# A fifth tile size with its own code, a packed word of sizes, and a block-wise end in a routed feed-forward kernel

## The chip, the core and the metric

The kernel runs on one core of one Trainium2 chip. Its engines are TensorE (PE in the profile; PEld is its weight loads), VectorE (DVE), ScalarE (ACT), GpSimd (POOL) and SyncE (SP). The metric is device time in microseconds of one execution.

## The reference, cut to what matters

2,048 tokens of 256 values are turned by one matrix that depends on two quaternions and a gate, sent each to the best of eight experts, and the expert's output is added to the token.

```python
def _L0_ffn_ref(x, router_w, router_b, w1, b1, w2, b2):
    logits = jnp.einsum('bsd,de->bse', x, router_w) + router_b
    top1 = jnp.argmax(jax.nn.softmax(logits, axis=-1), axis=-1)
    out = jnp.zeros_like(x)
    for i in range(8):
        h = jnp.einsum('bsd,df->bsf', x, w1[i]) + b1[i]        # 256 -> 2048
        a, g = jnp.split(h, 2, axis=-1)
        y = jnp.einsum('bsh,hd->bsd', a * jax.nn.sigmoid(g), w2[i]) + b2[i]   # 1024 -> 256
        out = out + jnp.where((top1 == i)[..., None], y, 0.0)
    return out
x = x + _L0_ffn_ref(_L0_cond_ref(x, cond_256, q_right, gate), ...)
```

Evaluated on the inputs that it draws, the reference's own routing gives the experts 308, 336, 181, 195, 258, 268, 327 and 175 tokens.

## The kernel before

**The prologue.** SP loads the tokens in four parts (x_loaded) and the first expert's w1. TensorE spreads the quaternions (the matmuls into late_ps, L971), turns the tokens in eight pairs of blocks (the loop over f, L976 to L993), computes the logits (L999), and then rotates all tokens, 256 at a time, in rotate_blocks(0) to rotate_blocks(7) (L1018). ScalarE copies each rotated pair out of PSUM, and SP writes it to the DRAM buffer x_rows (L349). In the midst of this VectorE picks the expert of each token and counts them (L758 to L765, in_row); two small matmuls (L1034, L1035) turn the counts into ranks, and VectorE makes one-hot rows (slot_one_hot, L768) from which TensorE sums the row indices (L1051). TensorE's instructions run in program order, so rotate_blocks(2) and later stand behind L1034, which waits for in_row. GpSimd then gathers the first expert's rows from x_rows (gather(0), L438) after it has waited for x_rows_written (all eight writes) and idx_ready (the indices).

**The tiles.** Each expert is one tile of up to 512 columns. Its TensorE code is leaf(size): first_product makes eight chunks c of the two halves a and g, each from six matmuls (fp32 split in a high and a low part), then second_half makes two halves of the output from 24 matmuls each: 96 + 48 = 144 matmuls a tile. There is one leaf for each of SIZES = (224, 272, 336, 512); at "top" a tree of branches (by_size) picks the smallest size that holds the expert's count. ScalarE (sigmoid, L579, and u_hi, L585) and VectorE (gated, L854, and lo_u, L860) work at the width of a block class instead: 224 for two blocks of 128, 336 for three, 512 for four. The output of a tile is biased by ScalarE into yt (L593), turned back in the next tile's code (turn_back, L1120), added to the rows by VectorE and scattered by GpSimd (L452).

**The sizes.** VectorE writes a table ctrl, and in its last element a word with three bits for each of tiles 1 to 7 and an end mark of SPECIAL = 4. TensorE waits for ctrl_ready, loads three elements of ctrl (L1065, L1082, L1084) and shifts the word by three bits a tile.

**The visits.** A visit(line) branches to a label elsewhere in TensorE's program, from where a branch leads straight back. There are six of them, five in the prologue behind the first; their labels stand in the prologue (1), ahead of "top" (2), in the leaves of 224 (3), 272 (4 and 5) and 336 columns (6). visit(1) is the first thing that TensorE does.

**The end.** After the last tile the word gives the end mark, and the code at "special" waits for both halves of yt, turns all of them back in eight transposes, and adds one to y_turned. VectorE then adds block after block (L883), and GpSimd scatters each. "special" then branches to "done".

Of the kernel before, what the change touches and what calls it, by code (L numbers as in the profile page):

```python
# [5 lines left out]
def adaln_moe_ffn_kernel(nc, x, cond, q_right, gate, router_w, router_b, w1, b1, w2, b2, out):  # L6
# [16 lines left out]
    P = 128  # L23
# [15 lines left out]
    SIZES = (224, 272, 336, 512)  # L39
# [16 lines left out]
    SPECIAL = len(SIZES)  # L56
# [8 lines left out]
    with ctx:  # L65
# [40 lines left out]
        ctrl = sb("ctrl", 3 + TAB, I32)  # L106
# [8 lines left out]
        places = sb("places", NE)  # L115
# [74 lines left out]
        turn_ps = pair[0] + pair[1]  # L190
        early_ps, late_ps = y_half
# [42 lines left out]
        ctrl_ready = sem("ctrl_ready")  # L234
        rot_x_ready = sem("rot_x_ready")
# [21 lines left out]
        y_turned = sem("y_turned")  # L257
        last_added = sem("last_added")
# [105 lines left out]
        def _(pool):  # L364
# [32 lines left out]
            for e in range(NE):  # L397
                nc.gpsimd.memset(places[:, e:e + 1], float(1 << (LEFT * (e - 1))) if e > 0 else 0.0)
# [106 lines left out]
        def _(act):  # L505
# [49 lines left out]
            for h in range(KH):  # L555
                act.sem_inc(yt_done[h], 1)
            act.sem_inc(sig_done[NC - 2], 1)
# [46 lines left out]
            def gate_tile(i, e, n):  # L604
# [35 lines left out]
        def _(dve):  # L640
# [164 lines left out]
            def indices(idx_ps, at, count):  # L805
# [13 lines left out]
            steps = sm[:, 6 * NE:7 * NE]  # L819
            bigger = ct[:, 0:NE * MORE].rearrange("p (e m) -> p e m", m=MORE)  # L820
# [5 lines left out]
            left = sm[:, 7 * NE + SPARE:7 * NE + SPARE + 1]  # L826
# [7 lines left out]
            V.memset(ctrl[:, 1 + TAB:2 + TAB], 0)  # L834
            link(V.tensor_tensor(places[:, :], places[:, :], steps, ALU.mult))
            link(V.tensor_reduce(left, places[:, :], AX.X, ALU.add))
            V.tensor_scalar(ctrl[:, 2 + TAB:3 + TAB], left, float(SPECIAL << (LEFT * (NE - 1))), None, ALU.add)\
                .then_inc(ctrl_ready, 1)
# [24 lines left out]
            def rows_of(i, first, count):  # L863

                return (pairs[buffer_of(i)].rearrange("p (s k h d) -> p s k h d", s=NSUB, k=2, h=KH)[:, first:first + count, 1],
                        y_ps[:, :].rearrange("p (h s d) -> p s h d", h=KH, s=NSUB)[:, first:first + count])

            def add_rows(i):

                for s in range(NSUB):  # L870
                    dve.wait_ge(gathered[s], (i + 1) * 16)
                dve.wait_ge(y_turned, i + 1)
                rows, y = rows_of(i, 0, NSUB)
                V.tensor_tensor(rows, y, rows, ALU.add).then_inc(y_done, 1)  # L874

            def add_last(i, blocks):

                for s in range(blocks):
                    dve.wait_ge(gathered[s], (i + 1) * 16)
                dve.wait_ge(y_turned, i + 1)  # L880
# [46 lines left out]
            for i in range(NE, TAB):  # L927
                with dve.If(last_tile >= i):
# [4 lines left out]
                    add_rows(i)  # L933

        @block.tensor
        def _(pe):
# [20 lines left out]
            def landing(line):  # L957
                here = nc.cur_bb
                pe.br(f"past{line}")
                nc.switch_bb(f"landing{line}", parent=visited_from[line])  # L960
                pe.nop()
                pe.br(f"back{line}")
                nc.switch_bb(f"past{line}", parent=here)

# [344 lines left out]
```

## Time and profile before

| | us |
|---|---|
| median of 3 runs (lowest, highest) | 208.42 (208.19, 209.0) |
| the profiled execution | 207.35 |
| its span | 205.6 |

An execution's time is its span and 1.75 us around it. The profiled execution lies 1.07 us (0.5%) below the median of the runs. In the rows below, a time is in microseconds from the span's start unless it says ns, PE rows are TensorE's matmuls, "q" behind an engine's name is its sequencer (branches, waits, register work), and [a <-b] behind an instruction is the idle time of its engine before it and what ended that. The matmuls' durations overlap, so their pitch is read from starts.

### The profile page before, as it was taken

Reading aid. Unit: us, or ns where it says so; the run is one execution under the profiler, and the core shown is the slowest. Engines: PE = TensorE matmul, PEld = TensorE weight load, DVE = VectorE, ACT = ScalarE, POOL = GpSimd, SP = SyncE. Lnnn points to the kernel's source line nnn. Section 1 sums busy time; section 2 is a strip of 40 time slices with the busy share of each in tenths; the row PEclk is TensorE's granted clock in tenths of the full one; section 3 lists DMA queues with packets and bytes.
Section 4 is the critical chain, followed back from the end, with each engine's and each line's share of the span. In section 5 each row is a group of like instructions: output and inputs, shape, how many; then the busy total and the mean of one; then the engine's idle time right before and its main releaser. Section 6 shows DMA issues by size and latency. Waiting matters only on the chain.

```text
span 205.6 us, 4304 instructions
## 1 busy us (share of the span) xinstructions
PE 191.6 (93%) x1451; PEld 181.2 (88%) x1453; DVE 146.1 (71%) x296; ACT 125.1 (61%) x222; POOL 87.7 (43%) x138
## 2 busy tenths in 40 slices
PE   7997867999999999999999999999999999999960
PEld 3777733999999999999999999999999999999950
DVE  4928944678854888398869869995999488839510
ACT  2454770385756676486875958695777667648310
POOL 8002544631700645445467084555637364004403
PEclk9999999999999999999999999999999999999997
DMA  4999925879948161787198469618861976001001
GB/s 136 383 402 385 311 64 190 261 260 328 308 128 357 51 213 47 249 333 238 34 390 302 154 199 406 232 38 303 344 205 53 336 277 208 0 0 37 28 5 43
DMA packets 20054, 42.34 MB, mean 206 GB/s; under 512 B 2472, under 2 KB 14905, under 8 KB 17978
## 3 DMA queue, kind: packets, MB, share of 16 engines
q1 hardware_dynamic: 15808, 31.54, 42.8%
q0 software_dynamic: 4000, 10.50, 16.1%
q8 instruction: 8, 0.13, 0.3%
q14 instruction: 20, 0.16, 0.2%
q10 hardware_dynamic: 218, 0.01, 0.1%
HBM read 35.74 MB, written 8.13 MB: 213 GB/s over the span
## 4 chain that ended last, share of the span: by engine, by line
PE 90%; DMA 4%; issue 1%; DVE 1%; POOL 1%; ACT 1%; DVEq 0%; POOLq 0%
PE y_ps L1208 8%; PE g_ps L1176 8%; PE g_ps L1169 8%; PE a_ps L1169 8%; PE y_ps L1210 8%; PE a_ps L1176 8%; PE y_ps L1209 8%; PE a_ps L1172 8%; PE g_ps L1172 8%; PE y_ps L1120 3%; PE y_ps L942 3%; DMA x_turn<-x_rows,g_idx 2%; PE a_ps L1018 2%; PE a_ps L1099 2%; DMA x_rows<-arena 2%
## 5 line engine op out<-in xcount | busy, mean ns | idle before, releaser
L854 DVE SCALAR_TENSOR_TENSOR arena<-a_ps,b_t,arena 128x336 f32<-128x336 f32 (+1 forms) x64 | 33.3, 521 | 27.7 <-PE a_ps L1176 24.1
L579 ACT ACTIVATE arena<-g_ps,b_t 128x336 f32<-128x336 f32 (+1 forms) x64 | 32.2, 503 | 32.4 <-PE g_ps L1176 32.2
L452 POOL DMA_INDIRECT out_dram<-x_turn,s_idx x22 | 28.5, 1295 | 47.3 <-DVE x_turn L874 35.4
L740 DVE TENSOR_TENSOR w_lo<-w_raw,w_hi 128x1024 fp32r<-128x1024 f32 x32 | 37.7, 1221 | 9.1 <-DMA x_turn<-x_rows,g_idx 5.2
L438 POOL DMA_INDIRECT x_turn<-x_rows,g_idx x24 | 30.6, 1275 | 31.1 <-DMA out_dram<-x_turn,s_idx 17.3
L1208 PE MATMUL y_ps<-u_hi,w_hi 128*128 128x336 f32 (+2 forms) x128 | 38.1, 298 | 0.3 <-issue 0.3
L1210 PE MATMUL y_ps<-u_lo,w_hi 128*128 128x336 f32 (+2 forms) x128 | 37.5, 293 | 0.0
L1209 PE MATMUL y_ps<-u_hi,w_lo 128*128 128x336 f32 (+2 forms) x128 | 37.5, 293 | 0.0
L1169 PE MATMUL g_ps<-xr_hi,w_hi 128*128 128x336 f32 (+2 forms) x128 | 36.1, 299 | 0.0
L1169 PE MATMUL a_ps<-xr_hi,w_hi 128*128 128x336 f32 (+2 forms) x128 | 35.6, 294 | 0.0
L1172 PE MATMUL a_ps<-xr_hi,w_lo 128*128 128x336 f32 (+2 forms) x128 | 35.5, 293 | 0.0
L1172 PE MATMUL g_ps<-xr_hi,w_lo 128*128 128x336 f32 (+2 forms) x128 | 35.5, 293 | 0.0
L585 ACT ACTIVATE u_hi<-arena 128x336 fp32r<-128x336 f32 (+1 forms) x64 | 28.4, 444 | 10.6 <-DVE arena L854 10.6
L528 ACT ACTIVATE w_hi<-w_raw 128x1024 fp32r<-128x1024 f32 x32 | 32.0, 1059 | 0.0
L860 DVE TENSOR_TENSOR u_lo<-arena,u_hi 128x336 fp32r<-128x336 f32 (+1 forms) x64 | 29.2, 456 | 1.2 <-ACT u_hi L585 0.5
L1176 PE MATMUL g_ps<-xr_lo,w_hi 128*128 128x336 f32 (+2 forms) x128 | 27.3, 294 | 0.0
L1176 PE MATMUL a_ps<-xr_lo,w_hi 128*128 128x336 f32 (+2 forms) x128 | 27.2, 293 | 0.0
L1208 PEld LDWEIGHTS y_ps<-u_hi,w_hi 128*128 128x128 f32 x128 | 24.2, 189 | 0.4 <-issue 0.4
L1169 PEld LDWEIGHTS g_ps<-xr_hi,w_hi 128*128 128x128 f32 x128 | 24.2, 189 | 0.3 <-issue 0.3
L1172 PEld LDWEIGHTS g_ps<-xr_hi,w_lo 128*128 128x128 f32 x128 | 24.3, 190 | 0.0
L1172 PEld LDWEIGHTS a_ps<-xr_hi,w_lo 128*128 128x128 f32 x128 | 24.3, 190 | 0.0
L1209 PEld LDWEIGHTS y_ps<-u_hi,w_lo 128*128 128x128 f32 x128 | 24.3, 190 | 0.0
(181 smaller groups left out, 306.8 us busy)
## 6 DMA issues: line engine op xcount, KB each, us to landing
w_raw<-in_L_ffn_w_dram SPq DMA_DIRECT2D x16, 1024.0 KB, 7.9
w_raw<-in_L_ffn_w_dram SPq DMA_DIRECT2D x16, 512.0 KB, 4.6
x_own<-in_x_dram SPq DMA_DIRECT2D x4, 512.0 KB, 6.0
x_rows<-x_own SPq DMA_DIRECT2D x4, 512.0 KB, 11.1
x_rows<-arena SPq DMA_DIRECT2D x8, 256.0 KB, 3.4
x_turn<-x_rows,g_idx POOLq DMA_INDIRECT x24, 6.0
out_dram<-x_turn,s_idx POOLq DMA_INDIRECT x22, 3.7
x_own<-x_rows,g_idx POOLq DMA_INDIRECT x8, 5.6
```

The lines of the kernel that those rows point to most:

```text
L438: nc.gpsimd.indirect_dma_start(out=pairs[buffer_of(i)][:, s * ROW:(s + 1) * ROW], out_offset=None, in_=x_rows, in_offset=bass.IndirectOffs ...
L528: nc.scalar.activation(unit_of(w1_hi, u), raw_unit(u), ACT.Copy)\
L579: nc.scalar.activation(sig[:, c % SIG_RING, 0:n], pair[c % RING][1][:, 0:n], ACT.Sigmoid, bias=b1_t[:, bass.ds(e * (2 * NC) + (NC + c), 1) ...
L740: V.tensor_tensor(unit_of(w1_lo, u), raw_unit(u), unit_of(w1_hi[:, :].bitcast(F32), u), ALU.subtract)\
L854: V.scalar_tensor_tensor(u32[:, c % (8 - SIG_RING), 0:n], pair[c % RING][0][:, 0:n], b1_t[:, bass.ds(e * (2 * NC) + c, 1)], sig[:, c % SIG ...
L860: V.tensor_tensor(u_lo[:, at:at + n], u32[:, c % (8 - SIG_RING), 0:n], u_hi[:, at:at + n].bitcast(F32), ALU.subtract).then_inc(u_lo_done[c ...
L1169: one = T.matmul(dst, w_part(w1_hi, k), xh, start=(k == 0), stop=False)
L1172: T.matmul(dst, w_part(w1_lo, k), xh, start=False, stop=False)
L1176: last = T.matmul(dst, w_part(w1_hi, k), xr_lo[:, k * ITEM:k * ITEM + n], start=False, stop=(k == KH - 1))
L1208: T.matmul(dst, w2_hi[:, wv], u_hi[:, uv], start=(c == 0), stop=False)
L1209: T.matmul(dst, w2_lo[:, wv], u_hi[:, uv], start=False, stop=False)
L1210: last = T.matmul(dst, w2_hi[:, wv], u_lo[:, uv], start=False, stop=(c == NC - 1))
```

## The change

- SIZES gets 320 between 272 and 336. TensorE has five leaves; the classes of width for ScalarE and VectorE stay 224, 336 and 512.
- The word of sizes holds all eight tiles, as 5 minus the size's number, with 0 as the end mark. VectorE makes it ahead of the rest of the table, from five small operations, before the one-hot rows for spare tiles (q_oh_spare); it signals packed_ready. TensorE loads this one word. It reads ctrl only in "special".
- visit(1) stays, with its label behind the leaf of 272 columns and so ahead of that of 320. The other five visits and their labels go. The five warming matmuls behind visit(1) go, and so do two of the four long ones ahead of the first tile.
- The two matmuls for wr_rot move from f == 4 to f == 6.
- rotate_blocks(2) and (3) move ahead of the matmuls that wait for in_row.
- At the end, ScalarE biases the first half of the output as soon as it is there, and the second half in two parts: 128 columns, signalled by yt_first, and the rest. TensorE turns the first half back (half_turned), and then the second half block by block, each block into a PSUM bank of its own. VectorE adds the first half for all blocks in one operation, and then the second half block by block.

```diff
-    SIZES = (224, 272, 336, 512)
+    SIZES = (224, 272, 320, 336, 512)
...
+    PLACES = [1 << (LEFT * e) for e in range(NE)]
...
+        apart = turn_ps[0:NSUB]
...
             def biased_rest(i, e, n):
...
                 if i >= NE - 1:
-                    for h in range(KH):
-                        biased(i, e, h, 0, FIRST, yt_done[h])
+                    biased(i, e, 0, 0, min(n, FIRST), yt_done[0])
+                    biased(i, e, 1, 0, P, yt_first)
+                    biased(i, e, 1, P, min(n, FIRST), yt_done[1])
...
             indices(early_ps[:, 0:FX], 0, FX)
-            subtile_one_hot(q_oh_spare, FX, TS - FX, q_spare).then_inc(q_oh_spare_ready, 1)
-
-            dve.wait_ge(spare_ready, 1)
...
             link(V.tensor_tensor(bigger, cnt.unsqueeze(2).to_broadcast([P, NE, MORE]), ...
             link(V.tensor_reduce(steps, bigger, AX.X, ALU.add))
+            link(V.tensor_tensor(places[:, :], places[:, :], steps, ALU.mult))
+            link(V.tensor_reduce(left, places[:, :], AX.X, ALU.add))
+            V.tensor_scalar(packed[:, :], left, float(len(SIZES) * sum(PLACES)), None, ALU.add).then_inc(packed_ready, 1)
+            subtile_one_hot(q_oh_spare, FX, TS - FX, q_spare).then_inc(q_oh_spare_ready, 1)
+
+            dve.wait_ge(spare_ready, 1)
...
+            def add_by_block(i, blocks, done):
...
+                dve.wait_ge(half_turned, i - NE + 2)
+                V.tensor_tensor(rows[:, 0:blocks, 0], y_half[0][:, 0:blocks * P].rearrange("p (s d) -> p s d", d=P),
+                                rows[:, 0:blocks, 0], ALU.add)
                 for s in range(blocks):
-                    rows, y = rows_of(i, s, 1)
-                    V.tensor_tensor(rows[:, 0], y[:, 0], rows[:, 0], ALU.add).then_inc(last_added, 1)
+                    dve.wait_ge(block_turned, (i - NE + 1) * NSUB + s + 1)
+                    last = V.tensor_tensor(rows[:, s, 1], apart[s][:, 0:P], rows[:, s, 1], ALU.add)
...
             visit(1)
             pe.wait_ge(still_set, 1)
-            keep_warm(early_ps, 5)
...
-                if f == 3:
-                    visit(2)
-                if f == 4:
+                if f == 6:
                     pe.wait_ge(wr_loaded, 16)
...
-                if g == 2:
-                    visit(3)
...
-            rotate_blocks(1)
+            for b in range(1, GROUPS):
+                rotate_blocks(b)
             pe.wait_ge(consts_ready, CONSTS)
             pe.wait_ge(in_row_ready, 1)
...
-            for b in range(2, NB // 2):
+            for b in range(GROUPS, NB // 2):
                 rotate_blocks(b)
-                if b == 5:
-                    visit(4)
...
-            visit(5)
...
             keep_warm_long(late_ps, 2)
-            pe.wait_ge(ctrl_ready, 1)
-            last_tile = load_last(pe)
-            visit(6)
-            keep_warm_long(late_ps, 2)
+            pe.wait_ge(packed_ready, 1)
...
-            pe.reg_load(word_reg, ctrl[0:1, 1:2])
-            pe.reg_mov(size_reg, f_size(reg(word_reg, 127)))
-            pe.reg_load(left_reg, ctrl[0:1, 2 + TAB:3 + TAB])
+            pe.reg_load(left_reg, packed[0:1, 0:1])
+            pe.reg_mov(size_reg, reg(left_reg, 1 << 30) & ((1 << LEFT) - 1))
+            pe.reg_mov(left_reg, reg(left_reg, 1 << 30) >> LEFT)
...
                     leaf(low)
                     here = nc.cur_bb
                     pe.br("top")
+                    if low == 1:
+                        landing_behind(1)
...
             nc.switch_bb("special", parent=begin)
             tile = reg(tile_reg, TAB)
-            turn_back_rows(NSUB)
+            pe.wait_ge(yt_done[0], at1)
+            for s in range(NSUB):
+                last = T.transpose(y_half[0][:, s * P:(s + 1) * P], yt[:, s * P:(s + 1) * P], ident[:, :])
+            last.then_inc(half_turned, 1)
+            for s in range(NSUB):
+                if s < 2:
+                    pe.wait_ge((yt_first, yt_done[1])[s], at1)
+                T.transpose(apart[s][:, 0:P], yt[:, ITEM + s * P:ITEM + (s + 1) * P], ident[:, :]).then_inc(block_turned, 1)
+            pe.wait_ge(ctrl_ready, 1)
+            last_tile = load_last(pe)
...
             first16 = pe.to_reg(reg(tile_reg, TAB) * 16 + 16)
+            pe.wait_ge(y_done, at1)
```

## Rows read from the trace of the kernel before

**Rows 1.** The page: busy time of TensorE; its granted clock in 40 slices.
```profile
PE 191.6 (93%) x1451; PEld 181.2 (88%) x1453; DVE 146.1 (71%) x296; ACT 125.1 (61%) x222; POOL 87.7 (43%) x138
PEclk9999999999999999999999999999999999999997
```

**Rows 2.** Groups by form, line L1208 at 336 columns.
```profile
L1208 PE MATMUL y_ps<-u_hi,w_hi 128*128 128x336 f32 x48 | 15.4, 320 | 0.0
```

**Rows 3.** Chain that ended last (start, us, what): chunks at 336, then at 272 columns.
```profile
44.53 0.31 PE g_ps L1176 x2
45.45 0.31 PE a_ps L1176 x2
...
125.02 0.25 PE g_ps L1176 x2
125.78 0.25 PE a_ps L1176 x2
```

**Rows 4.** Timeline of VectorE, the last chunk of tile 0.
```profile
51.32 0.57 DVE L854 SCALAR_TENSOR_TENSOR arena<-a_ps,b_t,arena 128x336 f32<-128x336 f32 x1 [0.55 <-PE a_ps L1176]
```

**Rows 5.** Timeline of TensorE at the wait for in_row.
```profile
17.96 0.17 PE L1034 MATMUL g_ps<-in_row,lower 128*128 128x8 bf16 x1 [1.36 <-DVE in_row L765]
```

**Rows 6.** Chain that ended last, from the rotations to the first gather.
```profile
20.94 0.89 PE g_ps L1018 x8
...
24.28 3.30 DMA x_rows<-arena
...
28.46 4.51 DMA x_turn<-x_rows,g_idx
```

**Rows 7.** Windows: length, busy PE, PEld, DVE, ACT, POOL, PEclk, DMA share, GB/s.
```profile
22.00:24.00 2.00, 2.00 (x18) 1.78 (x16) 2.00 (x10) 1.41 (x3) 1.57 (x5) 1.00 0.73 242
24.00:26.00 2.00, 1.07 (x17) 0.68 (x16) 1.88 (x10) 2.00 (x4) 0.00 (x0) 1.00 1.03 348
```

**Rows 8.** Timeline of VectorE from the ranks to the first indices.
```profile
18.46 0.17 DVE L777 COPY sm<-g_ps 128x8 f32<-128x8 f32 x1
...
21.73 3.60 DVE L768 TENSOR_SCALAR work<-iota,r_f,tok 128x128 f16<-128x128 bf16 x15
...
25.68 0.19 DVE L807 TENSOR_SCALAR g_idx<-y_ps 128x32 int32<-128x32 f32 x1
```

**Rows 9.** Three lines' instructions: branch durations in ns (min/median/max), first and last start.
```profile
L954 PEldq COMPARE_BRANCH  x5: 175/287/381, 7.1 to 29.1; - x5
L1261 PEldq COMPARE_BRANCH  x1: 3408/3408/3408, 198.3 to 198.3; - x1
L1245 PEldq COMPARE_BRANCH  x8: 169/169/184, 56.4 to 195.4; - x8
```

**Rows 10.** Timeline of TensorE at the start of the program.
```profile
1.50 2.31 PE L942 MATMUL y_ps<-still 128*128 128x512 bf16 x5 [1.50 <-DVE still L651]
3.75 1.03 PE L971 MATMUL y_ps<-ident,scratch 13*128 13x16 f32 x4
...
7.67 0.96 PE L983 MATMUL g_ps<-ident,x_own 128*128 128x128 f32 x4
8.46 0.63 PE L983 MATMUL a_ps<-ident,x_own 128*128 128x128 f32 x4
```

**Rows 11.** Chain that ended last, the end.
```profile
197.49 0.55 ACT yt L593
198.17 1.08 PE y_ps L1120 x8
199.38 0.43 DVE x_turn L883
...
200.08 0.98 POOL out_dram L452
```

**Rows 12.** Groups by form: ScalarE on 144 columns, VectorE on 128.
```profile
L721 DVE TENSOR_TENSOR scratch<-mask_j,coef_t 128x128 f32<-128x128 f32 x2 | 0.5, 290 | 0.0
...
L551 ACT ACTIVATE b_t<-y_ps 128x144 f32<-128x144 f32 x1 | 0.3, 285 | 0.0
```

More of the change, by code:

```diff
@@ L105, in adaln_moe_ffn_kernel @@
         s_idx = sb("s_idx", TAB * NSUB, I32)
-        ctrl = sb("ctrl", 3 + TAB, I32)
+        ctrl = sb("ctrl", 2 + TAB, I32)
+        packed = sb("packed", 1, I32)
+        places = sb("places", NE)
         ident = sb("ident", P)
@@ L397, in _ @@
             for e in range(NE):
-                nc.gpsimd.memset(places[:, e:e + 1], float(1 << (LEFT * (e - 1))) if e > 0 else 0.0)
+                nc.gpsimd.memset(places[:, e:e + 1], -float(PLACES[e]))
             for m, size in enumerate(SIZES[:-1]):
@@ L814, in _ @@
             indices(early_ps[:, 0:FX], 0, FX)
[L815 to L817 removed]
             MORE = len(SIZES) - 1
             steps = sm[:, 6 * NE:7 * NE]
+            left = sm[:, 7 * NE + SPARE:7 * NE + SPARE + 1]
             bigger = ct[:, 0:NE * MORE].rearrange("p (e m) -> p e m", m=MORE)
@@ L833, in _ @@
             V.tensor_scalar(ctrl[:, 1 + NE:1 + TAB], owner, float(MORE), None, ALU.add)
[L834 to L838, printed above, removed]
+            V.memset(ctrl[:, 1 + TAB:2 + TAB], 0).then_inc(ctrl_ready, 1)
             dve.wait_ge(idx_spare_summed, 1)
@@ L861, in lo_u, with rows_of @@
                                 u_hi[:, at:at + n].bitcast(F32), ALU.subtract).then_inc(u_lo_done[c], 1)
-            def rows_of(i, first, count):
-                return (pairs[buffer_of(i)].rearrange("p (s k h d) -> p s k h d", s=NSUB, k=2, h=KH)[:, first:first + count, 1],
-                        y_ps[:, :].rearrange("p (h s d) -> p s h d", h=KH, s=NSUB)[:, first:first + count])
+            def rows_of(i):
+                return pairs[buffer_of(i)].rearrange("p (s k h d) -> p s k h d", s=NSUB, k=2, h=KH)[:, :, 1]
             def add_rows(i):
@@ L1122, in turn_back, with turn_back_rows @@
                 return last
-            def turn_back_rows(blocks):
+            def turn_back_rows():
                 for h in range(KH):
                     pe.wait_ge(yt_done[h], at1)
-                turn_back(range(blocks)).then_inc(y_turned, 1)
+                turn_back(range(TURNED)).then_inc(y_turned, 1)
             def turn_back_rest():
@@ L1233, in leaf, with jump, by_size @@
                 second_half(size, 1)
-            def by_size(size, low, high):
-                if low == high:
-                    if low == SPECIAL - 1:
-                        with pe.If(size >= SPECIAL):
-                            here = nc.cur_bb
-                            pe.br("special")
-                            nc.switch_bb("behind_special", parent=here)
+            def jump(to, behind):
+                here = nc.cur_bb
+                pe.br(to)
+                nc.switch_bb(behind, parent=here)
+            def by_size(code, low, high):
+                if low == high:
                     leaf(low)
@@ L1248, in by_size @@
                 middle = (low + high + 1) // 2
-                with pe.If(size < middle):
-                    by_size(size, low, middle - 1)
+                with pe.If(code > len(SIZES) - middle):
+                    by_size(code, low, middle - 1)
                 with pe.Else():
-                    by_size(size, middle, high)
+                    if middle == high == len(SIZES) - 1:
+                        with pe.If(code < 1):
+                            jump("special", "behind_special")
+                    by_size(code, middle, high)
             begin = nc.cur_bb
@@ L1257, in _ @@
             tile = reg(tile_reg, TAB)
-            turn_back_rows(NSUB)
-            with pe.If(last_tile < tile):
-                here = nc.cur_bb
-                pe.br("done")
-                nc.switch_bb("behind_done", parent=here)
-            pe.reg_load(word_reg, ctrl[0:1, bass.ds(tile + 1, 1)])
-            pe.reg_mov(size_reg, f_size(reg(word_reg, 127)))
-            pe.reg_mov(left_reg, SPECIAL)
+            pe.wait_ge(yt_done[0], at1)
[8 more added lines that the diff above has]
+            last_tile = load_last(pe)
+            with pe.If(last_tile < tile):
+                jump("done", "behind_done")
+            pe.reg_mov(size_reg, 1)
+            pe.reg_mov(left_reg, 0)
             pe.reg_mov(held_reg, NE)
```

42 lines of the change are left out of this document (17 added, 25 removed).

## The prediction

> **What bounds the kernel now.** I read the page first. TensorE is busy for 93% of the span and stands at its higher clock level, 2.4 GHz, in 39 of 40 slices [rows 1]. The chain of waits then shows where that matters. From the first tile's first chunk to the last tile's last half it is TensorE alone, chunk behind chunk at an even pitch [rows 3], so a tile costs what its 144 matmuls cost, and all that VectorE, ScalarE and the queues do there is hidden. Only two stretches lie outside: the prologue, in which the chain goes from the rotations to the writes of x_rows to the gather [rows 6], and the end, in which it steps from ScalarE to TensorE, VectorE and GpSimd [rows 11]. The edits fall into these three places, and what one place gains is not lost again in another, since each is in series with the next.
>
> **The leaf of 320 columns.** The group at 336 columns has 48 matmuls of a kind that each tile runs 16 times (two halves by eight chunks), so three tiles run at 336 [rows 2]. They are the experts with 308, 336 and 327 tokens; only the first fits into 320. So one tile of eight changes its leaf. Its price from the pitch of six matmuls: 0.92 us at 336 columns (44.53 to 45.45) and 0.76 us at 272 (125.02 to 125.78) [rows 3], that is 0.0025 us a column for the six, 0.04 us for 16 columns, and 24 groups of six in a tile: 24 x 0.04 = **0.96 us less**. VectorE and ScalarE keep their width of 336 there. In the tile's last chunk VectorE still waited 0.55 us for TensorE [rows 4], while TensorE will come some 0.6 us earlier by then (sixteen groups by 0.04); so VectorE is just kept busy, and the second product's order gives the last chunk some 3 us more before it is read (seven of eight steps of three matmuls, half of 0.92 us each). I count the 0.96 in full; the lower bound is half of it.
>
> **Pairs 2 and 3 early.** TensorE stood idle for 1.36 us before L1034, waiting for in_row [rows 5]. Two pairs of rotations at 0.89 us [rows 6] fill this and 0.42 us more. So the last pair is done 1.36 us earlier, and the ranks come 0.42 us later. What does each end at? The writes of x_rows end at 27.58 (24.28 + 3.30), and the gather starts at 28.46 [rows 6]. The DMA engines were at a share of 0.73 in 22 to 24 us and at 1.03 right behind [rows 7]: 2 us x 0.30 = 0.6 us of transfers could move up, and not much more, since the engines are then full. By the GB/s of the two windows it would be (348 - 242) x 2 / 348 = 0.6 too. So the writes can gain about 0.65 us; the upper bound is that the last ones land quicker too, and they gain what the rotations do. The indices: after the ranks VectorE works without a pause to the first indices at 25.68 + 0.19 = 25.87 [rows 8]; with 0.42 us more that is 26.3, still ahead of 26.9.
>
> **One visit, and what goes with it.** The five visits that go cost the sequencer 0.18 to 0.38 us a branch [rows 9], next to matmuls that were queued or waits: I count nothing for them, nor for the table's loads that TensorE drops, since all of this ended before the gather landed (28.46 + 4.51). The visit that stays goes to a place behind two leaves. The trace of before has one branch to code that nothing had touched, the one to "done", and it took 3.41 us against 0.29 us for a visit [rows 9]. I take that: 3.1 us more at the very start. TensorE's first matmul was at 1.50, and L971 at 3.75, behind five warming matmuls of 2.31 us together [rows 10]. These go, and L971 can start at 1.50 + 3.1 = 4.6, so 0.85 us later; its followers (five warming matmuls, the turns) shift by as much. The clock softens this: the four transposes at 7.67 took 0.96 us and those at 8.46 took 0.63 [rows 10], so the step up from 1.2 to 2.4 GHz lay between. If it comes at the same time again, the turns that are 0.85 us late run mostly at the higher level, and only about 0.2 us is lost; if it comes 0.85 us later as well, all of it is. I take **0.6 us lost**. Bounds: nothing (the target is there already), and 1.5 us, if the step comes so late that some five groups more cost 0.33 us extra each. Moving the wr matmuls to f == 6 costs nothing, as the copies of the turned tokens wait for the same engine in either order; it keeps TensorE from waiting for rot_t, which is late by the same 0.85 us.
>
> **The start in sum.** The last rotation is 1.36 - 0.6 = 0.76 us earlier, the writes by the smaller of this and their own limit, **0.65 us**; the indices are at 25.87 + 0.42 + 0.6 = 26.9, level with the writes at 27.58 - 0.65 = 26.9. The gather, the turns and the first chunk follow in step. The bounds: 1.36 - 1.5, and with the ranks' 0.42 on top of 1.5 the indices at 27.8, so 0.2 us later; and 1.36 - 0.2, so 1.2 us earlier.
>
> **The word of sizes.** Five small VectorE operations now stand ahead of q_oh_spare, about 1 us, and so TensorE's sums for spare tiles and its two long warming matmuls come 1 us later. They end well before the gather lands. Nothing on the path; TensorE's sparse time grows, which is rival C.
>
> **The end.** Before: ScalarE's yt from 197.49 for 0.55, eight transposes from 198.17 for 1.08, VectorE's first block at 199.38 for 0.43, GpSimd's first scatter at 200.08 [rows 11]. After: the first half is biased long before, its transposes follow the last product directly, and VectorE adds it (256 columns, 0.43) at about 197.85 to 198.3. ScalarE's first 128 columns take 0.29 (144 columns took 0.285 [rows 12]) to 197.78. The steps between engines as before (0.13 us to TensorE, 0.13 to VectorE, 0.27 to GpSimd), one transpose 0.3, one block of 128 columns 0.29 [rows 12]: 197.78 + 0.13 + 0.3 + 0.13 = 198.34, + 0.29 + 0.27 = 198.90. **1.18 us less**, bounds 0.9 and 1.3. The second scatter follows the first at GpSimd's own pace. "special" then loads ctrl and branches to "done", again 3.4 us: until about 202.7, while the second scatter is issued from 200.2 on and has to land; hidden, though thinly.
>
> **The sum.** 0.65 + 0.96 + 1.18 = 2.8 us. Against the profiled execution 207.35 - 2.8 = 204.55; the runs' median lies 1.07 us above that execution, so 208.42 - 2.8 = **205.6 us**.
>
> **Rivals.**
>
> A. *The start gives nothing* (0.16). The step up of the clock comes a stage later: 1.5 us lost against 1.36 gained. 0.96 + 1.18 - 0.1 = 2.0 us: 206.4. For it: the step is the one thing in the rows whose time the kernel does not set. Against: the warming matmuls behind L971 remain.
>
> B. *320 is not worth 16 columns*, because VectorE, with no idle time left in tile 0, becomes the bound (0.05): 0.5 us of the 0.96 is lost, 206.1. Against it: TensorE reads the last chunk some 3 us later.
>
> C. *TensorE's clock falls before the first tile* (0.07). From the end of the rotations, about 22.5, to the long warming matmuls at about 28.7, it has only small matmuls, and two of the four long ones are gone. At the end of the trace, with the engine idle, the clock does fall (the last slice has 7 [rows 1]). Against: before, its idle gaps of 1.36 us and less brought no fall. Price: the turns, the warming matmuls between them and the first chunk at half pace, about 1.5 us: 207.1. The Trainium skill (TensorE: Matmul & The Clock Gate, Part 1: The HAM clock gate) has the low clock as the default state, which activity releases and an idle engine gets back; by that rule the thinner prologue is the risky edit here, and the trace agrees so far that the clock falls once the engine has nothing left.
>
> D. *The program no longer stays in TensorE's instruction memory* (0.09): slower. Five leaves instead of four, and five visits that touched them are gone. A branch to absent code costs 3.41 us [rows 9]. The sequencer takes the branch back to "top" at 195.4, 2.1 us before ScalarE gets the last result at 197.49 [rows 9, 11], so a miss at a tile's switch costs 3.4 - 2.1, about 1.4 us. Two misses eat the 2.8 us, from the third on it is slower; at all seven switches 7 x 1.4 = 9.8 us: 215.4. For it: the program grows by a quarter. Against: before, the chain goes from tile to tile within TensorE [rows 3], and a leaf of 272 columns runs for 24 x 0.76 = 18 us, in which the next stretch can come. The Trainium skill (Runtime: NRT & Kernel Launch, Instruction fetch mechanics) gives TensorE room for 2,048 instructions and says that a taken branch out of it stalls; five leaves of 288 matmul and load instructions and the some 600 others that ran before (1451 + 1453 less 8 x 288 [rows 1]) make 2,040 by estimate, and waits and branches come on top. By that page the misses are likelier than I make them; the trace shows only the one at "done".
>
> **The numbers.** The forecast has 0.63, A 0.16, B 0.05, C 0.07, D 0.09. A measurement of this kernel tells about 0.5%, 1.04 us, from no change. All but D are faster by more than that, but for the ends of A and C together: faster 0.85, same 0.06, slower 0.09. The range: best ends 1.2 + 1.0 + 1.3 = 3.5 us, 204.9, and the runs scatter some 0.3 us below their median: 204.6. Above, it takes in A and C up to 207.3, which leaves D and a little of C and of the lower side out.
>
> **What would show it.** L1034 without an idle time of 1.36 us before it; a branch of about 3.4 us at the start and L971 near 4.6; the gather near 27.8; one group of matmuls at 320 columns, 16 of a line, with a pitch of 0.88 us; the first scatter about 1.2 us nearer to the last product. Wrong would make it: gaps of TensorE between tiles (D), a granted clock below 1 after 8.5 us (C), or turns at the slow pace beyond 9.5 us (A).

## The result, and the profile after

The changed kernel takes 214.63 us (median of 4 runs, 213.8 to 215.34), the kernel before beside it 208.71 us (208.19 to 210.08): 1.0272 times as long, with an interval of 1.0209 to 1.0335. The forecast was 205.6 us, faster; the kernel became slower by 5.9 us between the medians. The profiled execution took 215.34 us, its span is 213.0 us, 7.4 us more than before.

The page of the changed kernel, its clock row and its row for the queue of instruction packets, q8 (packets, MB, share of the engines):

```profile
PE 193.0 (91%) x1443; PEld 182.9 (86%) x1443; DVE 146.4 (69%) x297; ACT 125.4 (59%) x223; POOL 87.4 (41%) x139
...
PEclk9999988757999999999999999999999999999997
...
q8 instruction: 11, 0.18, 0.4%
```

TensorE's work is about as before [rows 1], but the clock is below full in slices 6 to 10 (about 27 to 53 us), where it was not before. Instruction packets on q8 number 11; the page of before has 8 of them, 0.13 MB. In both the size is 16 KB a packet (0.18 MB by 11). The page doesn't say which engine's instructions they hold; where they fall is told below.

The rows of two lines of the changed kernel: L952, the branch of the one visit, and L1244, the branches of the tree that picks a leaf (durations in ns, min/median/max, first and last start):

```profile
L952 PEldq COMPARE_BRANCH  x1: 3489/3489/3489, 0.9 to 0.9; - x1
L1244 PEldq COMPARE_BRANCH  x21: 65/88/4638, 37.6 to 205.7; - x21
```

The first answers to the visits and to "done" [rows 9]: 3.49 us, as forecast. The second was not forecast. One of 21 branches takes 4.64 us, and it is the first, at 37.6 us: the way into the leaf of 320 columns for tile 0. In the trace, a packet of q8 starts inside each of the two long branches, at 1.84 and at 39.58 us.

The chain that ended last, of the changed kernel (start, us, what):

```profile
24.92 3.75 DMA x_rows<-arena
...
29.55 1.25 POOL x_turn L444
...
32.41 4.91 DMA x_turn<-x_rows,g_idx
37.37 0.33 PE a_ps L1095
...
38.45 4.07 issue
42.52 0.61 PE g_ps L1163
...
44.99 1.12 issue
46.11 0.43 PE a_ps L1163
...
206.94 0.45 PE y_ps L1258 x4
207.51 0.42 DVE x_turn L889
207.94 0.41 DVE x_turn L893 x2
208.41 0.98 POOL out_dram L458
```

The gather starts at 29.55, 1.09 us later than before [rows 6]; its third part lands at 37.32 (32.41 + 4.91), where the trace of before has 34.99. Then TensorE stands for 4.07 us with all its data there ("issue": nothing in the profile that it waits for), and again for 1.12 us inside the first chunk, right behind another packet of q8 (43.67 to 44.61). Windows of the changed kernel (columns as in [rows 7]; PEclk is the figure behind POOL's):

```profile
36.00:38.00 2.00, 0.63 (x4) 0.46 (x5) 1.14 (x1) 0.27 (x1) 0.00 (x0) 1.00 0.38 111
...
40.00:42.00 2.00, 0.00 (x0) 0.00 (x0) 0.27 (x1) 0.00 (x0) 1.67 (x2) 0.53 1.07 378
42.00:44.00 2.00, 1.48 (x6) 1.51 (x7) 0.00 (x0) 0.00 (x0) 1.43 (x2) 0.50 0.88 283
...
50.00:52.00 2.00, 2.00 (x15) 2.00 (x14) 1.45 (x3) 0.56 (x2) 1.50 (x2) 0.91 0.62 195
```

In the idle gap, at 40.1 us, the clock falls from 2.4 to 1.2 GHz, and tile 0 runs at half pace from its first product until about 50.4 us.

The account needs the third gather and the starts of tiles 0 and 1. Of the kernel before, GpSimd's and TensorE's timelines, and the third part's time from issue to landing; of the changed kernel, TensorE's timeline at tile 1 (its tile 0 is in the chain above):

```profile
31.32 1.00 POOL L438 DMA_INDIRECT x_turn<-x_rows,g_idx  x1 [0.30 <-issue]
...
36.14 0.39 PE L1169 MATMUL g_ps<-xr_hi,w_hi 128*128 128x336 f32 x1
...
59.14 0.32 PE L1169 MATMUL g_ps<-xr_hi,w_hi 128*128 128x336 f32 x1
```

```profile
DMA to landing us min/median/max: 3.7/3.7/3.7
```

```profile
68.61 0.32 PE L1163 MATMUL g_ps<-xr_hi,w_hi 128*128 128x336 f32 x1
```

Tile 0 starts at 42.52 in place of 36.14 (+6.38: 2.33 by the third gather, 4.05 by the gap). Tile 0 lasts 26.09 in place of 23.00 (+3.09). The other seven tiles last as long as before, within 0.03 us each. From the last product to the end of the span it is 6.06 in place of 8.17 (-2.11). The sum is +7.36 of the 7.38 by which the spans differ.

### The profile page after: what moved, and what is told of

It is laid out like the page before. It is cut to its first block, busy times and chain, and to the rows that moved or that the text cites. A ratio compares the mean times of both kernels' runs of the same rounds, so it can differ in the third digit from the quotient of the medians.

```text
span 213.0 us, 4271 instructions
## 1 busy us (share of the span) xinstructions
PE 193.0 (91%) x1443; PEld 182.9 (86%) x1443; DVE 146.4 (69%) x297; ACT 125.4 (59%) x223; POOL 87.4 (41%) x139
## 4 chain that ended last, share of the span: by engine, by line
PE 84%; DMA 8%; issue 4%; POOL 2%; ACT 1%; DVE 0%; SPq 0%; DVEq 0%; POOLq 0%
PE g_ps L1163 8%; PE a_ps L1163 8%; PE g_ps L1170 8%; PE a_ps L1166 8%; PE g_ps L1166 8%; PE a_ps L1170 8%; PE y_ps L1202 8%; PE y_ps L1203 8%; PE y_ps L1204 8%; DMA x_own<-in_x_dram 4%; DMA x_turn<-x_rows,g_idx 2%; PE y_ps L1116 2%; PE a_ps L1024 2%; DMA x_rows<-arena 2%; PE g_ps L1024 2%
## 5 line engine op out<-in xcount | busy, mean ns | idle before, releaser
L444 POOL DMA_INDIRECT x_turn<-x_rows,g_idx x24 | 29.9, 1247 | 30.0 <-DMA out_dram<-x_turn,s_idx 17.1
L1163 PE MATMUL g_ps<-xr_hi,w_hi 128*128 128x224 f32 (+3 forms) x128 | 36.7, 302 | 4.1 <-issue 4.1
L1202 PE MATMUL y_ps<-u_hi,w_hi 128*128 128x224 f32 (+3 forms) x128 | 38.0, 297 | 0.3 <-issue 0.3
L1204 PE MATMUL y_ps<-u_lo,w_hi 128*128 128x224 f32 (+3 forms) x128 | 37.4, 292 | 0.0
L1203 PE MATMUL y_ps<-u_hi,w_lo 128*128 128x224 f32 (+3 forms) x128 | 37.4, 292 | 0.0
L1163 PE MATMUL a_ps<-xr_hi,w_hi 128*128 128x224 f32 (+3 forms) x128 | 35.9, 296 | 1.1 <-issue 1.1
L1166 PE MATMUL a_ps<-xr_hi,w_lo 128*128 128x224 f32 (+3 forms) x128 | 36.0, 297 | 0.0
L1166 PE MATMUL g_ps<-xr_hi,w_lo 128*128 128x224 f32 (+3 forms) x128 | 36.0, 297 | 0.0
L1170 PE MATMUL g_ps<-xr_lo,w_hi 128*128 128x224 f32 (+3 forms) x128 | 27.6, 297 | 0.0
L1170 PE MATMUL a_ps<-xr_lo,w_hi 128*128 128x224 f32 (+3 forms) x128 | 27.5, 297 | 0.0
L1163 PEld LDWEIGHTS a_ps<-xr_hi,w_hi 128*128 128x128 f32 x128 | 24.8, 194 | 0.0
```

What stands on the lines that cost most here:

```text
L444: nc.gpsimd.indirect_dma_start(out=pairs[buffer_of(i)][:, s * ROW:(s + 1) * ROW], out_offset=None, in_=x_rows, in_offset=bass.IndirectOffs ...
L1163: one = T.matmul(dst, w_part(w1_hi, k), xh, start=(k == 0), stop=False)
L1166: T.matmul(dst, w_part(w1_lo, k), xh, start=False, stop=False)
L1170: last = T.matmul(dst, w_part(w1_hi, k), xr_lo[:, k * ITEM:k * ITEM + n], start=False, stop=(k == KH - 1))
L1202: T.matmul(dst, w2_hi[:, wv], u_hi[:, uv], start=(c == 0), stop=False)
L1203: T.matmul(dst, w2_lo[:, wv], u_hi[:, uv], start=False, stop=False)
```

## The experiments

Three theories were tried. *Not there*: a leaf's code has to be touched shortly before its use and in order; the five visits did that, and the one far visit doesn't. *Too large*: five leaves don't fit, whatever is visited. *Clock by itself*: the thinner prologue lets the clock fall. All ratios below are to runs of the kernel before on the same chip, with their intervals. The runs are spread over two chips, on which the median of the kernel before lies between 208.09 and 209.42 us, so kernels are compared by these ratios. Line numbers in rows are each kernel's own.

**e1_visits_back.** Visits 2 to 6 and the six labels back in the changed kernel:

```diff
+                if f == 3:
+                    visit(2)
...
+                if g == 2:
+                    visit(3)
...
+                if b == 5:
+                    visit(4)
...
+            landing(1)
...
+            visit(5)
...
+            visit(6)
+            LANDING_AT = {(0, 7): 3, (1, 2): 4, (2, 3): 6}
...
+                if size == 1:
+                    landing(5)
...
-                    if low == 1:
-                        landing_behind(1)
...
+            landing_behind(2)
```

> The changed kernel with the kernel before's visits 2 to 6 and their six labels put back (visit(1) again to a label in the prologue); five sizes, pairs, end and word as changed; none of the dropped warming matmuls. Theory 'not there' (the code of a leaf has to be touched shortly before, in the order in which the program runs; the one far visit at the start leaves nothing behind): no branch of 3.5 us at 0.9 us, no branch of 4.6 us ahead of tile 0, tile 0 back at 22 us (23.0 less 0.96), the prologue 3 to 4 us shorter than in the changed kernel; 205.6 to 207 us. Theory 'too large' (five leaves do not fit whatever is visited): the 4 us gap ahead of or in tile 0 stays, or moves to another tile; 210 us or more. Theory 'clock by itself' (the prologue is too thin without the warming matmuls): the branches are short again, yet the granted clock still falls before or in tile 0; 207 to 209 us.

205.35 us (204.64 to 205.81), ratio 0.9825 [0.9762, 0.9887]. The visits' branches in e1, and its clock row:

```profile
L971 PEldq COMPARE_BRANCH  x5: 168/287/1568, 6.9 to 28.6; - x5
...
PEclk9999966999999999999999999999999999999998
```

No visit but the last, beside the wait for the gather, takes longer than before [rows 9]; there is no gap of 4 us, and tile 0 starts at 36.39. *Too large* falls: five leaves, and 0.9825 where the changed kernel has 1.0272. *Not there* holds for tile 0. Its label 6, counted by the leaf's number, now stands in the leaf of 320 columns, tile 0's own, as it stood in tile 0's own leaf of 336 before. The leaf of 336, tile 1's, lies right behind that of 320 in the program; no visit touches it in e1, and tile 1 doesn't wait. The clock falls nevertheless (27.4 to 34.2 us).

**e2_visits_warm.** e1 with the dropped warming matmuls back:

```diff
+            keep_warm(early_ps, 5)
...
+            keep_warm_long(late_ps, 2)
```

> As the run before it (visits 2 to 6 back), and the five warming matmuls at the start and the two long ones ahead of the first tile put back as well. 'Not there': same as the run before within 0.5 us if the clock fell only because of the stall; 205 to 206 us. 'Clock by itself': 1.5 to 3 us faster than the run before, and the granted clock stays at 1.00 from 8.5 us on. 'Too large': no better than 210 us.

206.24 us, ratio 0.9887 [0.9848, 0.9927]: not faster than e1. The clock falls here too (26.1 to 32.9 us), so putting the dropped warming matmuls back doesn't keep it up.

**e3_no_visit.** The changed kernel without its visit:

```diff
-            visit(1)
...
-                    if low == 1:
-                        landing_behind(1)
```

> The changed kernel without its one visit; nothing put back. 'Not there': the visit bought nothing, so the gap of about 4 us ahead of tile 0's first product stays as it is, while the start is up to 3 us earlier: 211.5 to 213.5 us. If the visit did bring in part of the leaf, the gap grows by what it had saved, or a second one shows in another tile, and the time is 214 us or more. 'Too large' expects the gap as well, and says nothing on the start.

Three runs took 224.2 to 224.9 us and one 209.75; the profile is of one of the long ones (224.22). The tree's branches there:

```profile
L1241 PEldq COMPARE_BRANCH  x21: 65/92/7423, 34.3 to 214.8; - x21
```

Tile 0 waits for its leaf as in the changed kernel (4.27 us at 34.3), and tile 1 for its own, the 336, twice in a row (5.34 us at 62.2 and 7.42 at 67.6). So the one visit did not serve tile 0. In the long run that has a trace tile 1 is worse off without it, against "bought nothing"; e10 shows such a double wait again. The fourth run, 209.75 us, is close to the kernel before on that chip (209.42), with a mean granted clock of 0.973 against 0.934 to 0.939 in the three. It has no trace; it may be that such stalls differ from run to run of one kernel, and what the one visit was worth is left open by this.

**e4_no_512.** The changed kernel without the leaf of 512 columns:

```diff
-                    leaf(low)
+                    if low < len(SIZES) - 1:
+                        leaf(low)
```

> The changed kernel, with its one visit, but TensorE's code for tiles of 512 columns left out (no tile has that size with these inputs, so the work done is the same); the program is then about as long as before the change. 'Too large': with room for four leaves the branch ahead of tile 0 is short and the time falls to 206 to 208 us. 'Not there': length does not matter, the branch of 4.6 us ahead of tile 0 stays, 213 to 215.5 us.

213.25 us, ratio 1.0168 [1.0084, 1.0251]. The tree's branches:

```profile
L1245 PEldq COMPARE_BRANCH  x21: 65/88/4687, 37.5 to 204.8; - x21
```

The same stall with four leaves, as *not there* expected (213 to 215.5 us). *Too large* falls a second time.

**e9_far_before.** The kernel before, and of the whole change its visits alone:

```diff
-                if f == 3:
-                    visit(2)
...
-            landing(1)
...
-            visit(6)
...
-            LANDING_AT = {(0, 7): 3, (1, 2): 4, (2, 3): 6}
+            LANDING_AT = {}
...
+                    if low == 1:
+                        landing_behind(1)
...
-            landing_behind(2)
```

> The kernel before with its four sizes, prologue, pairs, warming matmuls and end, and only its visits changed: visit(1) goes to a label behind the leaf of 272 columns, the other five are gone. If the visits alone are the cause: a branch of about 3.5 us at 0.9 us, a branch of about 4.6 us ahead of tile 0 (now to the leaf of 336, the one behind the label), 211 to 214 us, 1.5 to 2.5 % slower than the kernel before. If the fifth leaf is needed for the loss: the start costs up to 1 us, tile 0 does not wait, 208.5 to 210 us.

214.43 us (213.86 to 215.36), ratio 1.0293 [1.0245, 1.0341]: the loss of the change, with four leaves and every warming matmul in place, and a little above the expected 211 to 214 us. The visit's branch, the tree's branches, and TensorE's timeline at the first product:

```profile
L935 PEldq COMPARE_BRANCH  x1: 3262/3262/3262, 0.9 to 0.9; - x1
L1240 PEldq COMPARE_BRANCH  x18: 65/77/4363, 38.1 to 205.2; - x18
```

```profile
42.76 0.62 PE L1160 MATMUL g_ps<-xr_hi,w_hi 128*128 128x336 f32 x1 [3.70 <-issue]
```

**e11_far_and_near.** e1 with the far label for visit(1):

```diff
-            landing(1)
...
+                    if low == 1:
+                        landing_behind(1)
```

> e1_visits_back with visit(1) to its far place again, that is the changed kernel with visits 2 to 6 put back. With e1 (near ones alone), the changed kernel (far one alone) and e3 (none) it makes a square. If the near visits decide: tile 0 does not wait, and what is left is the price of the far visit at the start, first rotations 1 to 1.5 us later than in e1, 206.5 to 208 us. If the far visit throws out what the near ones need: the branch of 4 us or more is there again, 210 us or more.

211.71 us, ratio 1.0146 [1.0091, 1.0201]. Neither theory: tile 0 doesn't wait, but the first near visit does, and the start is 6 us late. The near visits' branches, and TensorE's timeline at that one:

```profile
L971 PEldq COMPARE_BRANCH  x5: 174/289/6140, 8.4 to 35.3; - x5
```

```profile
15.00 1.10 PE L999 MATMUL a_ps<-ident,x_own 128*128 128x128 f32 x4 [4.16 <-issue]
```

Behind the far visit, visit(2) takes 6.14 us, where e1 has a short one; that the far visit takes away what the next one reaches for is the reading of this, not a thing that a row shows. In the square, the near ones alone have the ratio 0.9825, both 1.0146, the far one alone 1.0272, and none three long runs and one of 209.75 us (e3). The traces divide more plainly than the times: tile 0 waits for its leaf in the two without the near visits, and in neither of the two with them.

**e10_late_visit.** The changed kernel with its visit behind the last wait ahead of the tiles:

```diff
-            visit(1)
...
             pe.wait_ge(yt_set, 1)
+            visit(1)
```

> The changed kernel with its one visit moved from the start of the program to the last instructions ahead of the loop over the tiles, where TensorE waits for the gather. If what counts is that the code is touched shortly before its use: the 3.5 us leave the start (2 to 3 us won there), the same 3.5 us are paid next to the wait for the gather, and the branch ahead of tile 0 is short: 206.5 to 209 us. If code that is read in between, or the order of the visits, decides: the branch ahead of tile 0 takes 4 us or more all the same, 211 to 215 us.

219.21 us, ratio 1.0488 [1.0421, 1.0556]. The visit's branch, the tree's branches, and TensorE's timeline ahead of tile 1:

```profile
L971 PEldq COMPARE_BRANCH  x1: 3411/3411/3411, 29.1 to 29.1; - x1
L1244 PEldq COMPARE_BRANCH  x21: 65/92/7443, 35.2 to 209.4; - x21
```

```profile
57.96 0.31 PE L1204 MATMUL y_ps<-u_lo,w_hi 128*128 128x320 f32 x1
69.80 0.62 PE L1163 MATMUL g_ps<-xr_hi,w_hi 128*128 128x336 f32 x1 [11.53 <-issue]
```

Half of the theory held: 3.41 us next to the wait for the gather cost nothing, tile 0 starts at 36.10 and doesn't wait. Then tile 1 waits for 11.53 us, as in e3, and the time lies above both expected ranges. This late touch served tile 0's leaf and not tile 1's. With the visits of before and of e1 no tile waits.

**e6_320_and_end.** The kernel before with the fifth size and the end by block (the change's parts at biased_rest, add_by_block and "special"):

```diff
-    SIZES = (224, 272, 336, 512)
+    SIZES = (224, 272, 320, 336, 512)
...
+            def add_by_block(i, blocks, done):
```

> The kernel before with only the fifth size and the end by block; its visits, prologue, warming matmuls, pairs and word as before. The prediction's two other terms: tile 0 at 22.0 us in place of 23.0 and the first scatter 1.2 us nearer to the last product, 2.1 us less than the kernel before, clock at 1.00 up to the end. 'Too large' (five leaves do not fit): one tile or more starts 3 us late. If the start's edits were worth the 0.65 us of the prediction, e5 is that much faster than this one; if the pairs bring nothing because the writes end with the queue, both are the same within 0.3 us.

205.54 us (204.54 to 206.1), ratio 0.9837 [0.98, 0.9874]. Its clock fell as well, in 26.5 to 29.9 us, with the prologue of before, and tile 0 still starts at 36.12. No tile starts late, so *too large* falls here too. By the ratio it gains 3.4 us, where the two terms of the prediction sum to 2.1.

**e12_end_only.** e6 without the fifth size:

```diff
-    SIZES = (224, 272, 320, 336, 512)
+    SIZES = (224, 272, 336, 512)
```

> The kernel before with the end by block alone; four sizes. Predicted term: the first scatter 1.18 us nearer to the last product. The scatters' landing decides the rest: 1.2 us less in all if the last landing comes as long after its issue as before the change (3.5 us), about 2.3 us less if it comes after 2.3 to 2.6 us as in the changed kernel. 206 to 207.5 us; and e6 is 0.5 to 1 us faster than this, the worth of the fifth size.

205.76 us, ratio 0.9882 [0.9841, 0.9923], 2.3 us less than the kernel before it (208.09) by the medians, as expected where the last scatter lands sooner, and just under the range of 206 to 207.5 us. What the fifth size adds to it (0.5 to 1 us expected) is not settled by the times: the medians of e6 and e12 differ by 0.22 us, their ratios by 0.45%, and the intervals overlap. In the traces tile 0 takes 22.51 us in e6 and 23.44 in e12. Two rows on the last scatters, from issue to landing, of before and of e12:

```profile
DMA to landing us min/median/max: 2.8/3.2/3.5
```

```profile
DMA to landing us min/median/max: 2.3/2.5/2.8
```

**e5_warm_between.** e1 with warming matmuls in the thin stretch:

```diff
+            keep_warm(late_ps, 2)
             pe.wait_ge(b1_t_done, 1)
...
             pe.wait_ge(still32_set, 1)
+            keep_warm_long(late_ps, 3)
             pe.wait_ge(q_oh_spare_ready, 1)
```

> As e1_visits_back (visits 2 to 6 back), with warming matmuls in the two places where TensorE has little left: two bf16 ones behind the rotations, ahead of the wait for the biased b1, and three long ones ahead of the wait for q_oh_spare (the gap of 1.9 us in e1 and e2). Theory 'thin stretch' (the granted clock fell at 26 to 27 us in e1 and e2 because the rotations now end 1.5 us earlier against the indices and q_oh_spare comes 0.9 us later): the clock stays at 1.00 to the end, tile 0 takes 22.0 us, and its first product comes about 3.2 us after the first gather landed, as before the change, in place of 4.3 (e1): 1 to 1.5 us faster than e1. Theory 'no cost' (the warming and the gather hide the low clock): same as e1 within 0.5 us.

206.19 us, ratio 0.9862 [0.9824, 0.99]. The clock falls all the same (26.5 to 29.9 us), and there is no gain over e1. Since the warming did not keep the clock up, this says nothing on what the fall costs: "no cost" is not shown by it.

**e7_word_late.** e1 with q_oh_spare ahead of the word's five operations again:

```diff
+            subtile_one_hot(q_oh_spare, FX, TS - FX, q_spare).then_inc(q_oh_spare_ready, 1)
             MORE = len(SIZES) - 1
...
-            subtile_one_hot(q_oh_spare, FX, TS - FX, q_spare).then_inc(q_oh_spare_ready, 1)
```

> As e1_visits_back, with q_oh_spare written ahead of the five operations for the word of sizes, as before the change. 'Thin stretch' with the word as its cause: TensorE's gap ahead of the sums for spare tiles falls from 1.9 to about 1.0 us and the granted clock stays at 1.00 or falls later and for less long, 0.5 to 1.3 us faster than e1. With the pairs as its cause: the gap is shorter and the clock falls all the same, same as e1.

206.26 us, ratio 0.9883 [0.9838, 0.9929]. The gap shrank from 1.89 to 0.99 us, the clock fell later and for less long (27.4 to 30.8 us); the time is not better than e1's.

**e8_pairs_late.** e1 with one pair ahead of the wait for in_row:

```diff
-            for b in range(1, GROUPS):
-                rotate_blocks(b)
+            rotate_blocks(1)
...
-            for b in range(GROUPS, NB // 2):
+            for b in range(2, NB // 2):
```

> As e1_visits_back, with pairs 2 and 3 back behind the wait for in_row. 'Thin stretch' with the pairs as its cause: the rotations end near 24 us again, the clock stays at 1.00 in 24 to 34 us, and the first gather starts within 0.2 us of e1's, since the writes end with the queue either way: 0.5 to 1.3 us faster than e1. If the pairs' early place is worth the predicted 0.65 us: the gather starts 0.65 us later, and the time is 0.3 to 0.7 us more than e1's unless the clock gives it back.

206.03 us, ratio 0.9846 [0.9789, 0.9902]: no difference to e1. The clock fell later, at 33.0, and this once it touched the turns: tile 0 starts 1.94 us after the third gather has landed, where before it took 1.15.

The chain of e7, which has the pairs early and nearly the start of before, at the last pair and in two chunks of tile 0:

```profile
21.08 0.91 PE g_ps L1034 x8
...
22.01 0.61 ACT arena L554
...
22.75 4.52 DMA x_rows<-arena
...
28.15 4.42 DMA x_turn<-x_rows,g_idx
...
38.24 0.15 PE g_ps L1183
...
39.12 0.15 PE a_ps L1183
```

and VectorE's timeline of e7 in the last chunk of tile 0:

```profile
50.31 0.57 DVE L861 SCALAR_TENSOR_TENSOR arena<-a_ps,b_t,arena 128x336 f32<-128x336 f32 x1 [0.31 <-PE a_ps L1190]
```

They are read in the next section.

## Why the prediction was wrong, by its own steps

**The step that failed** is "The five visits that go cost the sequencer 0.18 to 0.38 us a branch ... I count nothing for them". It priced the visits by their branches and left out what they do. Short branches [rows 9] did not say that the visits were idle, but that each found its target there. The square shows what the near visits do: with them tile 0 has no gap, without them it has. e9 shows the whole edit of the visits by itself: without the five, and with the far one, the kernel before loses 2.9%. e1 shows the reverse: with the near ones the changed kernel is 1.75% faster than the kernel before. The far visit bears a part of the loss of its own, which the prediction, with 0.6 us lost at the start, didn't count either: beside the near ones it takes the ratio from 0.9825 to 1.0146, by the 6.14 us at visit(2) (e11). Which of the five near visits is needed was not tried. That e1's 205.35 us is so close to the forecast of 205.6 is in part luck: the term for the start was too large and that for the end too small, as told below, and e1 ran on a chip where the kernel before took 209.42 us. Against the kernel before, 1.3% was forecast.

**Rival D** (0.09) named the mechanism, code that TensorE has to wait for, with the wrong cause and the wrong place. The cause was "five leaves instead of four"; e4 has four leaves and stalls, e1 and e6 have five and don't. The place was every switch of tiles, 1.4 us each behind a running product; it was the first entry, at 37.6 us, where TensorE has nothing queued and the whole branch is seen. Its price there: 4.07 + 1.12 us of gaps, and 26.09 - 22.00 - 1.12 = 2.97 us for the half pace (22.00 is what tile 0 takes in e7, below). The rival's own difference was off as well: 3.4 - 2.1 is 1.3 us, not 1.4. The Trainium skill (Runtime: NRT & Kernel Launch, Instruction fetch mechanics) calls the instruction memory a FIFO that is filled sequentially in blocks of 16 KiB, and has a taken branch out of what was read ahead stall. The packets of 16 KB and the stalls in e4, e9 and e11 agree with that; which blocks each visit leaves behind, and why tile 1 waits twice in e3 and e10, no run here shows.

**The visit at the start** was priced rightly in itself: 3.49 us against 3.41, and the matmuls of before's L971 (now L979) at 4.79 against 4.6 forecast. The start behind it was mis-sized. The forecast had the gather 0.65 us earlier, near 27.8; it started at 29.55. TensorE's timeline of the changed kernel:

```profile
4.79 1.00 PE L979 MATMUL y_ps<-ident,scratch 13*128 13x16 f32 x4 [4.79 <-POOL sizes L406]
...
7.83 1.06 PE L991 MATMUL a_ps<-ident,x_own 128*128 128x128 f32 x4
8.69 0.95 PE L991 MATMUL g_ps<-ident,x_own 128*128 128x128 f32 x4
10.11 0.75 PE L991 MATMUL a_ps<-ident,x_own 128*128 128x128 f32 x4 [0.47 <-DMA x_own<-in_x_dram]
```

The clock stepped up at 9.4 us, against 8.4 before, as rival A has it: at 7.83 and 8.69 the turns are at the slow pace, where before those from 8.46 on are quick [rows 10]. On top, the second part of the tokens landed at 10.07 (7.00 before), which no term had. In the other kernels with the far visit it landed at 7.97 (e4), 8.38 (e11) and 7.14 (e9), in those without at 6.83 to 7.03. Why is open. In these four an instruction packet comes at 7.06 to 8.67 us, in before at 10.86; but all four start after 7.03 us, when the part has landed in the others, so they can't be what first held it up.

**Pairs 2 and 3** freed the rotations as forecast: in e7 the last write is issued at 22.75 in place of 24.28 [rows 6], and the idle time of [rows 5] is gone. But it takes 4.52 us in place of 3.30 and lands at 27.27 in place of 27.58 [rows 6]. Here 0.3 us are won, in e1 0.1, and none in e2 (27.64). The other kernels with the pairs early and no far visit at the start have 27.14 (e5), 27.19 (e10) and 26.48 (e3), those with the pairs late 27.41 to 27.83 (e6, e8). So one trace of each shows from nothing to 0.44 us of the forecast 0.65, and e3 alone more; in time e8, e6 and e1 can't be told apart.

**The leaf of 320** held. The pitch of six matmuls is 0.88 us in e7 (38.24 to 39.12), tile 0 lasts 22.00 us in place of 23.00, and VectorE still waits 0.31 us for TensorE in the last chunk [rows 4], so rival B falls. In e1 and e6 tile 0 takes 22.33 and 22.51 us: the two steps in its first chunk at which TensorE turns to xr_lo take 0.25 to 0.43 us each, where later ones take some 0.15. In e12, with 336 columns, it is the same (23.44 in place of 23.00), so it isn't the fifth size that costs this.

**The end** held for the first scatter and was under-sized in all. From ScalarE's start to the scatter: 206.98 to 208.41, 1.43 us in the changed kernel; 197.49 to 200.08, 2.59 us before [rows 11]: 1.16 us less, 1.18 forecast. e12 gains 2.3 us. The rest is the landing of the last scatter, 3.5 us after its issue before and 2.3 in e12. In the trace of before a 16 KB instruction packet runs from 202.45 to 203.66, behind the branch to "done" (198.3 to 201.7), while that scatter is on its way, and the scatter's last 4 KB packet follows it and ends at 204.1; in e6 the packet comes at 202.32, after the landing at 201.98. That the one delays the other is read from these times alone and not shown; e6's first scatter, with a packet beside it at 199.03, lands in 2.70 us.

**The clock** (rival C): ahead of tile 0 it fell in the profiles of the changed kernel and of all runs but e9, where it fell only in the gap, with and without the warming matmuls (e2, e5) and with the prologue of before (e6, e12), and cost 0.8 us at most where all visits are near: from the third gather's landing to tile 0 it is 1.96 us in e2, where eight long warming matmuls at half pace run until 34.07, and 1.34 in e6, against 1.15 before. The runs of the kernel before have mean granted clocks from 0.976 to 0.995, so it probably falls there at times as well. What cost time in the changed kernel was the fall in tile 0, behind the gap. In the Trainium skill (TensorE: Matmul & The Clock Gate, Part 1: The HAM clock gate) an idle engine gets the low clock back; the fall at 40.1 us inside the gap agrees.

**In sum**: e1 is the change without its fault, 1.75% faster than the kernel before. e6 can't be told from it (0.9837 against 0.9825) with two of the edits and the old start, so the fifth size and the end are the gain and the start's edits add nothing that can be measured. Both beat both kernels.

## What to carry to other kernels

An instruction that takes no time and seems to do nothing may be what makes another one short: before dropping it, ask what would be late without it, and look for a row in which the code had not been touched (here the 3.41 us branch to "done"). A stall of the instruction stream shows as idle time of an engine with "issue" as its releaser and a long branch beside it; price it at the place where the engine has nothing queued, with the clock's fall behind it. And of edits that come together, run the ones with sure terms first: two of them held all of the gain.

## What the runs showed of the hardware

The branches of TensorE that stalled took 3.26 us (the far visit of e9) to 4.69 us (the way into tile 0's leaf in e4), 6.14 us for a near visit behind a far one (e11), and 5.34 and 7.42 us in a row in e3; the median of the visits in e1 is 0.29 us. An instruction packet of 16 KB takes 0.88 to 2.05 us on its queue. In the trace of before no such packet starts between 54.16 and 199.24 us, while tiles 1 to 7 run three different leaves; so their code was there by then, if the packets are TensorE's, as those inside the long branches suggest.

The third part of the first gather took 4.91 us to land in the changed kernel, with a packet beside it from 34.76 us, and 4.81 in e9 with one at 35.09; in before, with none beside it, it took 3.67. But in e1 and e6 a packet ran beside it too, from 31.48 and 31.35 us, soon after its issue, and it took 3.93 and 3.63. So a packet beside it is not enough to delay it, and what does is open.
